# The depthwise convolution of a fused Mamba and MLP kernel on column halves of TensorE, with crossed copies by DMA

## The reference, cut to what matters

```
xp, res = split(ln(x) @ W_in.T)                       # 512 channels each
xc  = silu(conv(xp) + conv_b)                         # 4 taps, causal, each channel by itself
B, C, dt = split(xc @ W_x.T)                          # 16, 16 and 1 numbers for a token
dt  = softplus(dt * W_dt + b_dt)
h_t = exp(A * dt_t) * h_(t-1) + dt_t * B_t * xc_t     # 512 channels x 16 states
y_t = h_t . C_t + D * xc_t
x   = x + silu(y + res) @ W_out.T
h   = silu((ln(x) @ w1) * s1) * ((ln(x) @ w2) * s2)   # ternary weights, 1024 wide
h   = gelu((h @ h1) * t1);  h = gelu((h @ h2) * t2)
out = x + (h @ w3) * s3
```

## Time and profile before

| | us |
|---|---|
| median of 3 runs | 2713.77 (2713.58 to 2713.95) |
| the profiled execution, its own time | 2714.37 |
| its span in the trace | 2712.6 |
| PE, DVE, ACT, POOL busy | 2555.8, 2348.1, 2088.0, 2167.4 |
| mean granted TensorE clock | 0.983 |

### The profile page before, as it was taken

One profiled execution on the slowest core, in us unless ns is written; L12 is line 12 of the kernel. 1 busy time (PEld: TensorE's weight loads), 2 busy tenths in 40 slices (PEclk: granted clock), 3 DMA queues, 4 the chain that ended last, 5 costly groups with the idle time before them and its releaser, 6 DMA issues. The chain is left out here.

```text
span 2712.6 us, 52694 instructions
## 1 busy us (share of the span) xinstructions
PE 2555.8 (94%) x18562; PEld 2340.8 (86%) x18562; DVE 2348.1 (87%) x2767; ACT 2088.0 (77%) x4560; POOL 2167.4 (80%) x1694
## 2 busy tenths in 40 slices
PE   6779999999999999999999999999988999999999
PEld 4668888888888888888888888888877999999999
DVE  3999999999999999999999999999994277777776
ACT  6888887778888778888777788787767677777774
POOL 3788888888888888888888888888885586676663
PEclk8789999999999999999999999999989999999999
DMA  6112111211111112221112111211142222222220
GB/s 236 39 49 71 63 60 61 70 60 60 63 64 60 63 62 69 64 75 64 60 60 71 60 59 61 66 60 64 56 144 67 78 79 94 94 94 94 94 94 33
DMA packets 130188, 199.02 MB, mean 73 GB/s; under 512 B 16384, under 2 KB 93312, under 8 KB 129920
## 3 DMA queue, kind: packets, MB, share of 16 engines
q1 hardware_dynamic: 129920, 195.57, 22.0%
HBM read 144.68 MB, written 50.86 MB: 72 GB/s over the span
## 5 line engine op out<-in xcount | busy, mean ns | idle before, releaser
L1413 DVE TENSOR_TENSOR_SCAN h<-banks,ub 128x512 f32<-128x512 f32 x1024 | 1199.6, 1214 | 29.3 <-ACT banks L1212 28.5
L873 POOL TENSOR_TENSOR ub<-u,b_row 128x1020 f32<-128x1020 f32 x512 | 1216.0, 2375 | 0.1
L1426 DVE SCALAR_TENSOR_TENSOR acc<-banks,c_tok,acc 128x512 f32<-128x512 f32 x1024 | 725.5, 745 | 76.4 <-PE banks L1761 75.5
L1212 ACT ACTIVATE banks<-dt 128x510 f32<-128x510 f32 x1024 | 605.8, 596 | 124.2 <-DVE h L1413 118.8
L1761 PE MATMUL banks<-ident,h 128*128 128x128 f32 x4096 | 600.7, 279 | 91.2 <-DVE acc L1426 50.4
L1761 PEld LDWEIGHTS banks<-ident,h 128*128 128x128 f32 x4096 | 480.8, 143 | 180.9 <-DVE h L1413 104.6
L1749 PE MATMUL banks<-act_high,h_rounded 128*128 128x256 f32 x2048 | 515.5, 291 | 7.0 <-POOL act_low L900 5.5
L1749 PE MATMUL banks<-act_low,h_rounded 128*128 128x256 f32 x2048 | 495.2, 281 | 0.0
L1749 PEld LDWEIGHTS banks<-act_high,h_rounded 128*128 128x128 f32 x2048 | 387.8, 189 | 13.9 <-issue 13.3
L1749 PEld LDWEIGHTS banks<-act_low,h_rounded 128*128 128x128 f32 x2048 | 388.2, 190 | 0.1
L872 POOL TENSOR_TENSOR ub<-b_u,enter 128x4 f32<-128x4 f32 x512 | 106.2, 207 | 257.7 <-DVE h L1413 253.1
(11 more groups left out here) (155 smaller groups left out, 5520.3 us busy)
## 6 DMA issues: line engine op xcount, KB each, us to landing
b_row<-b_scratch SPq DMA_DIRECT2D x128, 512.0 KB, 3.9
z_scratch<-z_out SPq DMA_DIRECT2D x128, 256.0 KB, 2.1
zl_raw<-z_scratch SPq DMA_DIRECT2D x32, 1024.0 KB, 6.8
x_sb<-in_x SPq DMA_DIRECT2D x32, 256.0 KB, 4.3
x_res<-in_x SPq DMA_DIRECT2D x32, 256.0 KB, 3.3
h_full<-in_h SPq DMA_DIRECT2D x2, 4096.0 KB, 18.2
x_scratch<-x_sb SPq DMA_DIRECT2D x32, 256.0 KB, 2.7
out_e<-x_scratch SPq DMA_DIRECT2D x16, 512.0 KB, 3.9
```

The lines of the kernel that those rows point to most:

```text
L873: nc.gpsimd.tensor_tensor(ub[:, n % 2, :, 1:], u[:, :, 1:], b_row[:, n // QUARTER % 2, n % QUARTER:n % QUARTER + 1, 1:].to_broadcast([P, E ...
L1212: nc.scalar.activation(decay_half(k)[:, :, 1:], dt[:, par, 2 * i:2 * i + 2, 1:], ACT.Exp, scale=rate[n]).then_inc(decay_ready, 1)
L1413: nc.vector.tensor_tensor_scan(h[:, n % 2, 2 * i:2 * i + 2].rearrange("p e t -> p (e t)"), banks[:, k % DECAYS, :], ub[:, n % 2, 2 * i:2 * ...
L1426: nc.vector.scalar_tensor_tensor(out=acc[:, par, q], in0=turned[q], scalar=c_tok[:, par, q, n:n + 1], in1=acc[:, par, q], op0=ALU.mult, op ...
```

## The change: what it does

`xp` gets a fourth dimension, half h = 0 or 1, which belongs to channels 0 to 63 or 64 to 127 of each tile. In `xp[:, e, h]` the 64 partitions of the half's own side ("straight") hold its 64 channels as before, and the 64 partitions of the other side ("crossed") hold the same channels shifted by one token. One product then sums two taps of 64 channels: 128 rows, 64 columns of weights, 256 tokens; two products (b = 0, 1; token offset 2b) make the four taps. Half 0 writes PSUM partitions 0 to 63 and half 1 partitions 64 to 127. The number of products stays (four for each tile).

ACT copies each `xp` job in two instructions of 64 partitions each instead of one. SP then waits for both and issues two DMAs from SBUF to SBUF, each of 64 partitions x 2 tiles x 256 tokens (128 KB), for each of the two jobs; the convolution waits for them. DVE builds `conv_diag` of 16 blocks 128 x 64 from `folded`, a sum of the two halves of the identity. The host reorders `conv_w`. `conv0` and `conv1` are whole pieces now, at PE's steps 0 and 1. Nearly all steps of the tables are new, and some waits are added that the new order needs.

```diff
-        conv_diag = sb("conv_diag", [P, ET, TAPS, P], where=a_only)
+        conv_diag = sb("conv_diag", [P, ET, 2, TAPS // 2, HP], where=a_only)
-        xp = sb("xp", [P, ET, HALO + T], where=a_only)
+        xp = sb("xp", [P, ET, 2, HALO + T], where=a_only)
...
-            norm={29: ('xn', 'xp0.a'), 31: ('xp0.b', 'xp1.a', 'xp1.b')},
-            front={0: ('conv0.a',), 1: ('conv0.b',), 2: ('conv0.c', 'conv0.d'), 3: ('conv1.a', 'conv1.b'), 4: ('conv1.c',), 5: ('conv1.d',), 10: ('ssm.a',), 11: ('ssm.b',), 13: ('dtc',), 23: ('acc0.a', 'acc0.b', 'acc0.c'), 25: ('acc1.a', 'acc1.b', 'acc1.c')},
-            post={10: ('gT0',), 13: ('gT1',), 14: ('out.a',), 16: ('out.b',), 17: ('out.c', 'out.d')},
-            mlp={32: ('yn',), 51: ('uu0.a', 'uu0.b'), 52: ('uu1.a', 'uu1.b'), 54: ('uu2.a', 'uu2.b', 'uu3.a', 'uu3.b', 'gg0.a'), 57: ('gg0.b', 'gg1.a', 'gg1.b'), 59: ('gg2.a', 'gg2.b', 'gg3.a'), 61: ('gg3.b',), 71: ('h0.a', 'h0.b', 'h0.c'), 72: ('h0.d', 'h1.a'), 73: ('h1.b', 'h1.c'), 75: ('h1.d',), 78: ('h2.a', 'h2.b'), 80: ('h2.c', 'h2.d'), 82: ('h3.a',), 83: ('h3.b', 'h3.c', 'h3.d')})
-        DVE_AT = dict(gated=(88, 88, 90, 93))
-        ACT_AT = dict(sums=4, x1=22, sums2=24, logs=6, logs2=28, xn=31, xp=(2, 5), silu=(10, 26), ssm=16, z=18, soft=21, acc=(27, 31), gT=17, high2=40, high=(66, 66, 67, 70), z_out=(77, 80, 85, 89), a_dt=31)
-        POOL_AT = dict(low2=21, x1=11, normalize=9, normalize2=17, dt=14, u=15, low=(33, 36, 34, 35))
-        SP_AT = dict(x=0, x1=12, res=12, write_b=4, b=(11, 14, 1, 6), z_out=(35, 40, 41, 44))
+            norm={27: ('xn',), 28: ('xp0.a',), 29: ('xp0.b',), 31: ('xp1.a', 'xp1.b')},
+            front={0: ('conv0',), 1: ('conv1',), 4: ('ssm.a',), 6: ('ssm.b',), 12: ('dtc',), 23: ('acc0.a',), 24: ('acc0.b',), 25: ('acc0.c', 'acc1.a'), 26: ('acc1.b',), 27: ('acc1.c',)},
+            post={6: ('gT0',), 7: ('gT1',), 10: ('out.a',), 11: ('out.b',), 13: ('out.c',), 19: ('out.d',)},
+            mlp={43: ('yn',), 52: ('uu0.a',), 53: ('uu0.b', 'uu1.a', 'uu1.b', 'uu2.a'), 55: ('uu2.b', 'uu3.a', 'uu3.b'), 56: ('gg0.a', 'gg0.b'), 58: ('gg1.a', 'gg1.b'), 60: ('gg2.a',), 61: ('gg2.b',), 62: ('gg3.a',), 63: ('gg3.b',), 66: ('h0.a',), 67: ('h0.b', 'h0.c'), 71: ('h0.d',), 72: ('h1.a',), 73: ('h1.b', 'h1.c'), 74: ('h1.d',), 77: ('h2.a',), 78: ('h2.b',), 79: ('h2.c',), 80: ('h2.d',), 81: ('h3.a', 'h3.b'), 82: ('h3.c',), 83: ('h3.d',)})
+        DVE_AT = dict(gated=(84, 88, 93, 96))
+        ACT_AT = dict(sums=14, x1=24, sums2=32, logs=19, logs2=37, xn=31, xp=(0, 2), silu=(7, 26), ssm=9, z=16, soft=19, acc=(31, 31), gT=10, high2=48, high=(59, 66, 67, 68), z_out=(78, 80, 85, 88), a_dt=31)
+        POOL_AT = dict(low2=25, x1=14, normalize=14, normalize2=22, dt=11, u=15, low=(32, 33, 34, 34))
+        SP_AT = dict(crossed=(0, 0), x=0, x1=12, res=12, write_b=4, b=(9, 13, 2, 5), z_out=(37, 38, 41, 42))
...
+            def cross(c, j):
+                rows = slice(2 * j, 2 * j + 2)
+                sp.wait_ge(straight_ready[j], 2 * (c + 1))
+                sp.dma_start(xp[HP:P, rows, 0, HALO - 1:HALO - 1 + T], xp[0:HP, rows, 0, HALO:HALO + T]).then_inc(crossed_in[j], 16)
+                sp.dma_start(xp[0:HP, rows, 1, HALO:HALO + T], xp[HP:P, rows, 1, HALO - 1:HALO - 1 + T]).then_inc(crossed_in[j], 16)
...
             for name, src in (("w1", w1), ("w2", w2), ("h1", h1)):
                 sp.dma_start(full[name][:], src.rearrange("(k p) n -> p k n", p=P)).then_inc(early_in, 16)
+            for j in range(2):
+                cross(0, j)
             write_b(0)
...
+                    for j in range(2):
+                        if n == SP_AT["crossed"][j] and to_front is not None:
+                            cross(to_front, j)
...
-                take(f"xp{j}", c, xp[:, 2 * j:2 * j + 2, HALO:], bank(f"xp{j}", c).rearrange("p (e t) -> p e t", e=2))
+                wait_full(act, f"xp{j}", c)
+                rows = bank(f"xp{j}", c).rearrange("p (e t) -> p e t", e=2)
+                for half in range(2):
+                    at = HALO - half
+                    last = nc.scalar.activation(xp[HP * half:HP * (half + 1), 2 * j:2 * j + 2, half, at:at + T], rows[HP * half:HP * (half + 1)], ACT.Copy)
+                    last.then_inc(straight_ready[j], 1)
...
-                        for tap in range(first_tap, first_tap + TAPS // 2):
-                            last = nc.tensor.matmul(into[:, i * T:(i + 1) * T], conv_diag[:, e, tap], xp[:, e, tap:tap + T],
-                                                    start=(tap == 0), stop=(tap == TAPS - 1))
+                        pe.wait_ge(crossed_in[j], 32 * (c + 1))
+                        for i in range(2):
+                            e = 2 * j + i
+                            for b in range(TAPS // 2):
+                                for h in range(2):
+                                    last = nc.tensor.matmul(into[HP * h:HP * (h + 1), i * T:(i + 1) * T], conv_diag[:, e, h, b], xp[:, e, h, 2 * b:2 * b + T],
+                                                            start=(b == 0), stop=(b == TAPS // 2 - 1))
```

More of the change, by code:

```diff
@@ L32 @@
 P = 128
+HP = P // 2
 EPS = 1e-5
@@ L43, in program @@
     DI = w_out.shape[0]
-    TAPS = conv_w.shape[-1]
+    TAPS = 4
     NS = a_log.shape[0]
@@ L244, in program @@
         halo_ready = sem("halo_ready")
+        straight_ready = [sem(f"straight_ready{j}") for j in range(2)]
+        crossed_in = [sem(f"crossed_in{j}") for j in range(2)]
+        fold_done = sem("fold_done")
         soft_step = sem("soft_step")
@@ L695, in mlp @@
             def mlp(c, s):
-                if s in SP_AT["z_out"]:
-                    store_z(c, SP_AT["z_out"].index(s))
+                for p in range(PAIRS):
+                    if s == SP_AT["z_out"][p]:
+                        store_z(c, p)
             for c in range(CHUNKS):
@@ L896, in mlp @@
                     nc.gpsimd.tensor_tensor(xT_low[:], xT[:], xT_high[:].bitcast(F32), ALU.subtract).then_inc(xT_low_ready, 1)
[L897 to L901 removed]
+                for p in range(PAIRS):
+                    if s == POOL_AT["low"][p]:
+                        pool.wait_ge(act1_high_ready, PAIRS * c + p + 1)
+                        nc.gpsimd.tensor_tensor(act1_low[c % 2][:, 2 * p:2 * p + 2], silu1[:, p], act1_high[c % 2][:, 2 * p:2 * p + 2].bitcast(F32),
+                                                ALU.subtract).then_inc(act1_ready, 1)
             bodies(norm, front, scan, post, mlp, lambda: None, NS)
@@ L1049, in norm @@
                 if n == ACT_AT["xn"]:
+                    if c >= 1:
+                        wait_full(act, "xp1", c - 1)
+                        wait_full(act, "acc1", c - 1)
                     take("xn", c, xnT[:].rearrange("p k t -> p (k t)"), bank("xn", c))
@@ L1054, in project @@
                     wait_full(act, "xp0", c)
-                    nc.scalar.activation(xp[:, :, 0:HALO], xp[:, :, T:T + HALO], ACT.Copy, scale=keep(c)).then_inc(halo_ready, 1)
-                    act.wait_ge(halo_ready, c + 1)
-                take(f"xp{j}", c, xp[:, 2 * j:2 * j + 2, HALO:], bank(f"xp{j}", c).rearrange("p (e t) -> p e t", e=2))
+                    if c >= 1:
+                        wait_full(act, "conv1", c - 1)
+                    for k in range(2):
+                        after(act, crossed_in[k], 32 * c)
+                    rows = xp[:].rearrange("p e h t -> p (e h) t")
+                    nc.scalar.activation(rows[:, :, 0:HALO], rows[:, :, T:T + HALO], ACT.Copy, scale=keep(c)).then_inc(halo_ready, 1)
+                    act.wait_ge(halo_ready, c + 1)
+                wait_full(act, f"xp{j}", c)
[4 more added lines that the diff above has]
+                    last.then_inc(straight_ready[j], 1)
+                act.wait_ge(straight_ready[j], 2 * (c + 1))
+                act.sem_inc(freed(f"xp{j}", c), 1)
             def front(c, n):
@@ L1133, in silu_conv @@
             def silu_conv(c):
+                after(act, u_ready, c)
+                if c >= 1:
+                    wait_full(act, "ssm", c - 1)
+                    wait_full(act, "acc1", c - 1)
                 for j in range(2):
@@ L1380, in make_diagonals @@
                 dve.wait_ge(weights_in, 16 * 10)
+                nc.vector.tensor_tensor(folded[:], ident[:, 0:HP], ident[:, HP:P], ALU.add).then_inc(fold_done, 1)
+                dve.wait_ge(fold_done, 1)
                 for e in range(ET):
-                    for k in range(TAPS):
-                        nc.vector.tensor_scalar(conv_diag[:, e, k], ident[:], conv_w_sb[:, e, k:k + 1], None, ALU.mult)
+                    for h in range(2):
+                        for b in range(TAPS // 2):
+                            nc.vector.tensor_scalar(conv_diag[:, e, h, b], folded[:], conv_w_sb[:, e, h, b:b + 1], None, ALU.mult)
                     last = nc.vector.tensor_scalar(d_diag[:, e], ident[:], d_sb[:, e:e + 1], None, ALU.mult)
```

29 lines of the change are left out of this document (14 added, 15 removed).

## The result

The kernel after takes 2692.8 us (median of 4 runs, 2691.1 to 2694.1), the kernel before beside it 2713.9: a ratio of 0.992 [0.990, 0.994]. The forecast was 2686. The profiled execution took 2691.05 us, its span is 2689.3.

What follows compares the result with a forecast made beforehand. It took PE pieces between transpose groups to bound the kernel, 2.2 us a body deep, over a DVE floor of 60.1. From 2714.4: -43 for bodies, +15 for the start, 2686.4; median 2686, range 2668 to 2705.

Steps and rivals of the forecast that it cites:

- Rival 1: Convolution on PE: the column halves run one after the other, convolution stays 6.9 us a body; 2741 us, chance 12%.
- 3.5 us a body saved: Convolution on PE: paired records on two column halves take 0.109 us each instead of 0.217; 0 if they don't overlap.
- The new stall around the second silu visit: DVE at ACT's second silu visit: 7.2 us to the next decay against 6.76 us of DVE work, stall 0.44 us.
- 28.6 x 1.5 = 43 us: Steady stretch: DVE's waits fall from 2.84 to 1.3 us a body, 1.5 us saved in each of 28.6 bodies.
- hidden by 0.8 us: Crossing of xp1 in a body: lands at 1056.5, PE reaches conv1 at 1057.3, so no wait; crossings' cost 0.
- Rival 3: Crossings land late in each body, by 4.3 us; PE waits 1.4, DVE gets some 0.9; 2712 us, chance 7%.
- Rivals 2 and 5: POOL and ACT take most of the gain, 2718 us, 16%; or DVE's waits vanish but for silu visits, 2675, 5%.
- Rival 5: Steady bodies: DVE's waits vanish but for the silu visits, gaining 54 us; 2675 us, or 2660 with unheld start; 5%.
- Behind it come the same 19.3, and 1.3 for `sums`: Start: from chunk 0's convolution to first scan 19.3 us as before, plus 1.3 for chunk 1's later sums; scan at 57.5.
- chunk 1's crossing lands behind them: PE has a wait of 3 us where it had 2.6, so I add 0.4: Start: chunk 1's crossing queues behind weights h2 and w3 (5 MB), costing PE 0.4 us more waiting.
- Rival 4: Start: crossings aren't held by the weights, since DMA engines serve short transfers in between; 2673 us, chance 10%.
- The tail: Second phase and tail: no convolution, and pieces keep their order apart from new steps, so change taken as 0.

## Why the prediction was right, and where it was not

**The sign and the size** were right, 7 us off, but that is partly luck: two misses of 12 and 13 us stood against each other.

**Rival 1, the halves don't overlap,** is out: two records start 6 to 11 ns apart. The rule of the Trainium skill on which it rested, "TensorE: Matmul & The Clock Gate", Part 3 (The mechanism), that a load overlaps only a matmul of another row group, does not hold here: both halves use all 128 rows. The Trainium skill, "TensorEngine Tiling (Array Packing)", Key Properties, says that a change of the tiling mode drains the engine; no run here sets such a drain apart, but the trace has room for it. A piece takes 1.88 us where eight pairs at 0.216 are 1.73, and the first of its records starts 0.20 us after the transpose record ahead of it, where transposes follow each other at 0.11. The step "3.5 us a body saved" measures 6.94 - 2 x 1.88 = 3.2.

**The steady state** had the right mechanism (DVE is the floor, and its waits shrink), but was mis-sized, and its parts are not those forecast. Waits fell from 2.8 to 1.1 us a body where 1.3 was predicted. But the prediction had DVE's waits for ACT rise from 0.58 to about 1.0 and those for PE fall to 0.3; they are 0.27 and 0.85. The new stall around the second silu visit came, as 0.52 at gate 0 (0.44 predicted), but its releaser is PE's product and not ACT's decay, of which only 0.2 to 0.3 us lie hidden beneath it. POOL is at 0, as forecast. That the sum comes near 1.3 is luck in part. The term of the sum, "28.6 x 1.5 = 43 us", measures 55.5: bodies 1 to 30 are 1.85 us shorter each. The count, 30 for 28.6, makes only 2 us of the difference. The rest is in the size of 1.5: the gate's silu over the whole run shows 1.78 and the median body 2.03.

**What the prediction ascribed to PE's load** holds only with the tables. It had PE at 56.9 us a body, which "no longer bounds"; with the halves alone PE has that slack and the body stays at 63.28, since the slack lies at steps 0 to 5, where PE waited for DVE already, and DVE waits at steps 14 to 20. It costed the tables by their effect on the lumps and never asked what they would do without the room, or the room without them.

**Crossings in a body** land in 2.4 us, as predicted (page, part 6), but they are not "hidden by 0.8 us": PE waits for them in every body, 0.46 us, which the prediction named as a sign of being wrong. The term 0 holds for the time all the same, since DVE has nothing of that wait, as the run without crossings shows. Rival 3 is out.

**Rivals 2 and 5.** POOL and ACT don't take the gain (no row of POOL, 0.27 us for ACT). Rival 5 had the gain of bodies, 54 us, and not the path: DVE's waits for PE didn't vanish.

**The start** was the failed step. "Behind it come the same 19.3, and 1.3 for `sums`": 32.67 + 5.65 to 60.40 are 22.1, not 20.6, and the convolution began 1.3 later than the 31.4 taken: +17.5 for the first scan where +14.6 was predicted. With the halves and the old tables that stretch is 19.4 (39.93 to 59.32), so the 2.8 us more are the new tables', of which the prediction saw only `sums`. Worse is "chunk 1's crossing lands behind them: PE has a wait of 3 us where it had 2.6, so I add 0.4". PE waited 7.3 us and DVE 9.9 + 3.6; body 0 is 10.7 us longer. The prediction saw the transfer behind h2 and w3 and gave it 0.4 us, without working out when the queue would come to it. The run with the crossings first takes 7.7 of it away by the queue's order alone; the halves with the old tables, in the old order, have 2.7 us in place of 10.7. Rival 4, that short transfers are served in between, is out; its 2673 for a start that isn't held is near that run's 2671, by the same cancelling: its bodies gain 54.0 us, and start and tail lose 10.7.

**The tail** was taken at 0 and is 3.9 us longer. By the mark of the table above, 710.5 us before, it is 714.6 with the halves alone, 716.2 with the tables alone and 715.8 in the kernel before with its few finer steps. Its parts say more. The last body's scans take 4.2 us less than before. From the last scan's end to the first piece of the second phase on DVE are 104.5 us before and 112.3 after, and 113.5 with the tables alone, but 108.0 with the halves alone. The second phase itself differs by 0.3. So most of the loss comes with the new tables, at the passage between the phases, where the granted clock is 0.85 to 0.96, so at the lower level for a part of the time. What in them does it, no run shows.

## What to carry to other kernels

Time saved on an engine is worth nothing where that engine waits for the others already: look up at which steps the bounding engine waits, and if the saving isn't there, work has to be moved into it; try each half of such a change alone, for both can be worth zero and their product everything. A transfer that is new on a shared in-order queue waits for whatever stands ahead of it, so at a start put the small ones that the chain needs ahead of the weights: that was two moved loops and some 21 us here, as much as the change itself. A piece moved in a hand-written table lands beside other pieces, and shares banks with steps far away: two local moves that looked sensible cost 1.2 and 1.35 us a body here, so count what stands at every step of the new table before a run, and read from the run whether the waits are still in their old places.
